# Attention value products with two heads in one strip of 32 rows, and two transposes per block in place of four

## Chip, cores and metric

The kernel runs on one core of a Trainium2 chip. The metric is device time in microseconds (us) of one execution. Engines: PE is TensorE (matmuls; PEld is its weight loads), DVE is VectorE, ACT is ScalarE, POOL is GpSimd, SP is SyncE, which issues most DMAs.

## The reference, cut to what matters

`x` has the shape 16 x 256 x 128 and is float32. Three layers follow one another: half a mixture-of-experts layer (8 experts, 2 per token), an attention layer, and the same half expert layer again.

```
x = x + 0.5 * ffn(layernorm(x))
x = x + attention(layernorm(x))
x = x + 0.5 * ffn(layernorm(x))

# attention: 16 heads of 8 values, chunks of 64 queries; each looks at its own chunk's keys and the chunk before
scores = einsum('bcqhd,bckhd->bchqk', qc, kc) * scale
attn   = softmax(where(valid, scores, -1e9))
out    = einsum('bchqk,bckhd->bcqhd', attn, vc) @ Wo.T + bo
```

## The kernel before, in words

The 4096 tokens are 32 tiles of 128 tokens (`T` = 32). Both expert layers (`ffn(0)`, `ffn(1)`) sort the tokens by expert through DRAM. Between them stands the attention, a software pipeline over the 32 tiles, here called blocks, with `T + TAIL` = 39 iterations of `attend(i)` on each engine. The order of work on each engine is written out by hand, and semaphores join the engines. Two blocks are one sequence (`TS` = 2): t even is its first block, t odd its second.

PE's iteration i (L785) goes, in this order:

1. `round_one(i)` (L637): scores of block i+1 for the strips 2 and 3 (L624) and transposed scores of block i-1 (L628). It waits for `m01_ready`, so that the maxima of the last scores are read out of PSUM, and for `p01_ready`.
2. `small_moves(i)` (L719): three 128x128 products or transposes (L724, L727, L730), one of which transposes `OS`, the finished heads' output of block i-3.
3. `values(i-2)` (L761): the value products of block i-2.
4. `round_two(i)` (L656, lines L628 and L634), `router_part(i)` (L740: in three of four iterations a piece of the second router, with the lines L518, L526 or L535; all of them write the same PSUM bank `M1`, after a wait for `pvs_ready`), and `round_three(i)` (L670, lines L634 and L624).
5. `stage(i)` (L698): values, queries and keys of a sequence to come (L705, L711 or L716, L717).
6. `to_tokens(i-2)` (L733): after a wait for `pvs_ready`, four 128x128 transposes (L737) from `PVS` into `M1`.

The value products: the probabilities `PT` lie with keys on the 128 partitions and queries along the free dimension, and the values `VM` are the stationary operand. In `VM` each head owns 32 columns: 8 values, a one (whose product is the sum of the probabilities), and 23 zeros. A product of a head therefore gives 32 rows of PSUM, of which 9 are used. `M1` is one PSUM bank of 512 columns. Head b*4+h writes the rows of strip h (32h to 32h+31) and the columns of b (128b to 128b+127), so that 16 heads fill the bank. An even block takes 16 matmuls of 128 columns (L780), an odd one 32 of 64 columns (L782); four consecutive ones go to the four strips.

ACT then copies `M1` (128x512) to `PVS` (L975), PE transposes its four squares back into `M1` (L737), and DVE's `divide` (L1280) takes the reciprocals of the 16 sums (L1285) and multiplies (L1286) into `OS`, which raises `os_ready`. `values` of the next block waits for `os_ready`.

DVE's iteration (L1289): `maxima(i, 0)` (L1278) after `round_three`, `divide(i-3)`, at some iterations the combination of the first expert layer's results (L1250) or parts of the router, `maxima(i+1, 2)` (L1278) after `round_one` of the next iteration, the rest of that work, and the residual addition (L1325). ACT's iteration (L959): the copy of the small moves (L964), at some iterations normalised rows (L942) or a copy of rows (L880), the copy to `PVS` (L975), the exponentials (L922) in two halves, and copies for `stage`.

Of the kernel before, what the change touches and what calls it, by code (L numbers as in the profile page):

```python
# [24 lines left out]
P = 128  # L25
# [4 lines left out]
H, DH, W = 16, 8, 64  # L30
C = L // W
TS = L // P
ROWS32 = 32
HG = P // ROWS32
HQ = H // HG
KINDS = 4
QRING = 6
KRING = 3
# [28 lines left out]
def need(eng, sem, value):  # L67

    if not (isinstance(value, int) and value <= 0):
        eng.wait_ge(sem, value)  # L70
# [31 lines left out]
def macaron(nc, x, wq, bq, wk, bk, wv, bv, wo, bo, rscale, rw, experts, pes, consts, picks, out):  # L102
# [8 lines left out]
    with ExitStack() as ctx:  # L111
        def sb(name, shape, dt=F32):
            return ctx.enter_context(nc.sbuf_tensor(name, shape, dt))

        def sem(name):
            return ctx.enter_context(nc.semaphore(name))
# [11 lines left out]
        o = 0  # L128
# [4 lines left out]
        IDN, BEFORE, ONES, HMASK, IOTA, REG0, KTH, SIOTA, TRI, SROW, TOKEN, FROW = parts  # L133
# [6 lines left out]

        VM = sb("VM", [P, KRING, 3, H * ROWS32])
        MB = [sb(f"MB{i}", [P, P]) for i in range(2)]
        PT = [sb(f"PT{i}", [P, HG, KINDS * P]) for i in range(2)]
        MOP = [sb(f"MOP{i}", [P, 3, P]) for i in range(2)]
        PVS, RD, OS = sb("PVS", [P, HG, P]), sb("RD", [P, H]), sb("OS", [P, H, DH])
        CW = sb("CW", [P, T, TOPK])
        NHALF, REPS, EULER = sb("NHALF", [P, T]), sb("REPS", [P, T]), sb("EULER", [P, T])
        FILL = sb("FILL", [P, FILLERS, D + 1])
# [44 lines left out]
        ABANK = [PS[:, i, :] for i in range(2)]  # L193
        BBANK = [PS[:, 2 + i, :] for i in range(HG)]
        M0, M1 = PS[:, 6, :], PS[:, 7, :]
        EARLY = PS[:, 4, :]

        ROUTER = [PS[:, 4, :], PS[:, 5, :], PS[:, 6, :]]
# [40 lines left out]
        p01_ready, p23_ready, pv_done, pvs_ready = sem("p01_ready"), sem("p23_ready"), sem("pv_done"), sem("pvs_ready")  # L239
        to_done, os_ready, res_done = sem("to_done"), sem("os_ready"), sem("res_done")  # L240
# [27 lines left out]
        def two_halves(bank, v):  # L268
            return bank[:, v * P:(v + 1) * P].rearrange("p (a q) -> p a q", q=W)

        def moved(i):


            return [n for n, t in enumerate((i, i - 3, i - 4)) if blk(t)]
# [92 lines left out]
        def _(pool):  # L367
# [6 lines left out]
            pool.wait_ge(vm_zeroed, 1)  # L374
            pool.memset(VM[:, :, :, :].rearrange("p s w (h c) -> p (s w h) c", c=ROWS32)[:, :, DH:DH + 1], 1.0)\
                .then_inc(vm_zeroed, 1)
# [134 lines left out]
        def _(pe):  # L511
# [29 lines left out]
            def ffn(ph):  # L541
# [50 lines left out]
                for s in range(WRITTEN[ph] * XRING):  # L592
# [3 lines left out]
                    if ph == 0 and s in (10, 12, 14):  # L596
                        i = s // 2 - 9
                        stage_bank_free(i)
                        stage(i, EARLY)
                with pe.Fori(WRITTEN[ph], n // XRING - 1) as i:  # L600
# [6 lines left out]
            def strip(a):  # L607
                return slice(a * ROWS32, (a + 1) * ROWS32)

# [5 lines left out]
            def own_twice(t, a):  # L615
                return K[strip(a), t // TS % KRING, 0:W].unsqueeze(1).broadcast_to([ROWS32, 2, W])

# [68 lines left out]
            def stage_bank_free(i):  # L686


                s, odd = i // TS + 1, i % TS
                if odd:  # L690
                    if seq(s + 1):
                        pe.wait_ge(xat_ready, s + 2)
                    elif seq(s):
                        pe.wait_ge(v_ready, s + 1)
                elif seq(s):
                    pe.wait_ge(k_ready, s + 1)

            def stage(i, bank=M0):  # L698


                s, odd = (i + 1) // TS + 1, (i + 1) % TS
                if odd:
                    if seq(s):
                        for a in range(TS):
                            ins = pe.matmul(bank[:, a * P:(a + 1) * P], XAT[:, a * P:(a + 1) * P], WV[:, :],  # L705
                                            start=True, stop=True)
                    if seq(s + 1):
                        if (s + 1) * TS % TG == 0:
                            pe.wait_ge(xa_ready, (s + 1) * TS // TG + 1)
                        for a in range(TS):  # L710
                            ins = pe.transpose(bank[:, L + a * P:L + (a + 1) * P], XA[:, (s + 1) * TS % TG + a, :], IDN)  # L711
                    if seq(s) or seq(s + 1):
                        ins.then_inc(vx_done, 1)
                elif seq(s):
                    pe.wait_ge(xat_ready, s + 1)
                    pe.matmul(bank[:, 0:L], WQ[:, :], XAT[:, :], start=True, stop=True)  # L716
                    pe.matmul(bank[:, L:2 * L], WK[:, :], XAT[:, :], start=True, stop=True).then_inc(qk_done, 1)  # L717
# [15 lines left out]
            def to_tokens(t):  # L733

                pe.wait_ge(pvs_ready, t + 1)
                for b in range(HG):
                    ins = pe.transpose(M1[:, b * P:(b + 1) * P], PVS[:, b, :], IDN)  # L737
                ins.then_inc(to_done, 1)

            def router_part(i):  # L740
# [20 lines left out]
            def values(t):  # L761


                s, a = t // TS, t % TS
                pe.wait_ge(p23_ready, t + 1)
                if a == 0:
                    pe.wait_ge(v_ready, s + 1)
                else:
                    pe.wait_ge(vm_ready[s % KRING], 16 * 2 * (s // KRING + 1))
                need(pe, os_ready, t)  # L770
                for b in range(HG):
                    p = PT[t % 2][:, b, :].rearrange("p (r h q) -> p r h q", r=2, q=W)
                    out = two_halves(M1, b)
                    for r in (None,) if a == 0 else (0, 1):
                        w = 0 if a == 0 else 2 if r == 0 else 1
                        for h in range(HQ):
                            o = (b * HQ + h) * ROWS32
                            v = VM[:, s % KRING, w, o:o + ROWS32]
                            if r is None:
                                ins = pe.matmul(out[strip(h), :, :], v, p[:, :, h, :], start=True, stop=True)  # L780
                            else:
                                ins = pe.matmul(out[strip(h), r, :], v, p[:, r, h, :], start=True, stop=True)  # L782
                ins.then_inc(pv_done, 1)

            def attend(i):  # L785
# [86 lines left out]
        def _(act):  # L872
# [9 lines left out]
            def ffn(ph):  # L882
# [21 lines left out]
                for s in range(written):  # L904
# [3 lines left out]
                    if ph == 0 and s in (11, 13, 15):  # L908
                        stage((s - 1) // 2 - 9, EARLY)
                with act.Fori(written // RING, n // RING - 1) as i:  # L910
# [33 lines left out]
            def attention_rows(g, half=None):  # L944

                act.wait_ge(lnshift_ready, g + 1)
                for a in range(TG) if half is None else range(half * TG // 2, (half + 1) * TG // 2):
                    ins = normalised(XA[:, a, :], g * TG + a, LN, a)
                if half != 0:
                    ins.then_inc(xa_ready, 1)  # L950
# [8 lines left out]
            def attend(i):  # L959
                if moved(i):  # L960
                    act.wait_ge(mt_done, i + 1)
                    need(act, res_done, i - 5)
                    parts = slice(moved(i)[0] * P, (moved(i)[-1] + 1) * P)
                    act.copy(MOP[i % 2][:, :, :].rearrange("p n q -> p (n q)")[:, parts], M0[:, parts]).then_inc(mt_ready, 1)  # L964
                if i == 0:
                    attention_rows(1)
                if (g := group(i, 5)) is not None:
                    attention_rows(g)
                if (g := group(i, -8)) is not None:
                    router_inputs(g)  # L970
                if (g := group(i, -9)) is not None:
                    second_rows(g)
                if blk(i - 2):
                    act.wait_ge(pv_done, i - 1)
                    act.copy(PVS[:, :, :].rearrange("p b q -> p (b q)"), M1).then_inc(pvs_ready, 1)  # L975
                if blk(i - 1):
                    act.wait_ge(r2_done, i)
                    probabilities(i - 1, 0).then_inc(p01_ready, 1)
                if (g := group(i, -8)) is not None:
                    router_rows(GROUPS + g, M1, XNT[:, :])  # L980
                if blk(i - 1):
                    act.wait_ge(r3_done, i + 2)
                    probabilities(i - 1, 1).then_inc(p23_ready, 1)
                stage(i)
# [47 lines left out]
        def _(dve):  # L1032
# [247 lines left out]
            def divide(t):  # L1280


                dve.wait_ge(to_done, t + 1)
                o = M1.rearrange("p (h c) -> p h c", c=ROWS32)
                step(dve.reciprocal(RD[:, :], o[:, :, DH]))  # L1285
                dve.tensor_tensor(OS[:, :, :], o[:, :, 0:DH], RD[:, :].unsqueeze(2).broadcast_to([P, H, DH]),  # L1286
                                  ALU.mult).then_inc(os_ready, 1)
# [222 lines left out]
```

## Time and profile before

| what | us |
|---|---|
| median of 3 runs (lowest to highest) | 640.94 (639.59 to 642.64) |
| the profiled execution's own time | 640.15 |
| its span, first to last instruction | 638.1 |
| PE busy | 520.2 (82%) |
| PE weight loads busy | 457.1 (72%) |
| DVE busy | 416.4 (65%) |
| ACT busy | 277.3 (43%) |
| POOL busy | 363.3 (57%) |

By the trace the attention's value products run from 235.9 to 455.8 us. Before them lie the first router and expert layer, and behind them the second expert layer and the last combination. "Idle before" in a row is the time for which the engine did nothing ahead of the instruction, and the arrow names who ended it; "issue" means that the profile shows nobody. Rows of one engine can overlap, since matmuls are pipelined.

### The profile page before, as it was taken

Reading aid. Unit: us, or ns where it says so; the run is one execution under the profiler, and the core shown is the slowest. Engines: PE = TensorE matmul, PEld = TensorE weight load, DVE = VectorE, ACT = ScalarE, POOL = GpSimd, SP = SyncE. Lnnn points to the kernel's source line nnn. Section 1 sums busy time; section 2 is a strip of 40 time slices with the busy share of each in tenths; the row PEclk is TensorE's granted clock in tenths of the full one; section 3 lists DMA queues with packets and bytes.
Section 4 is the critical chain, followed back from the end, with each engine's and each line's share of the span. In section 5 each row is a group of like instructions: output and inputs, shape, how many; then the busy total and the mean of one; then the engine's idle time right before and its main releaser. Section 6 shows DMA issues by size and latency. Waiting matters only on the chain.

```text
span 638.1 us, 20679 instructions
## 1 busy us (share of the span) xinstructions
PE 520.2 (82%) x7242; PEld 457.1 (72%) x7243; DVE 416.4 (65%) x1431; ACT 277.3 (43%) x627; POOL 363.3 (57%) x425
## 2 busy tenths in 40 slices
PE   0899865999999599999999899999730999999920
PEld 0666635899999478888788778878520999999920
DVE  5776653666676857677688887656324566766747
ACT  0444112443443246666566657555420344434404
POOL 8777775775566431343657565561667556656630
PEclk9999896999999679999899999999855899999975
DMA  9611222222322312010212111120102222323259
GB/s 268 206 48 54 68 70 51 84 71 83 83 82 75 100 51 66 23 52 20 76 30 76 35 40 33 44 55 19 34 27 77 72 81 85 83 74 92 83 143 277
DMA packets 60136, 49.37 MB, mean 77 GB/s; under 512 B 8736, under 2 KB 53536, under 8 KB 59936
## 3 DMA queue, kind: packets, MB, share of 16 engines
q1 hardware_dynamic: 51872, 31.51, 18.6%
q0 software_dynamic: 8192, 16.86, 8.0%
q8 instruction: 50, 0.82, 0.5%
q14 instruction: 22, 0.18, 0.1%
HBM read 23.55 MB, written 20.59 MB: 69 GB/s over the span
## 4 chain that ended last, share of the span: by engine, by line
PE 57%; DVE 13%; POOL 10%; issue 8%; DMA 5%; ACT 3%; SPq 3%; DVEq 0%; POOLq 0%; ACTq 0%
PE PS L560 16%; PE PS L574 7%; PE PS L634 7%; POOL xs_rows L408 6%; PE PS L628 5%; DVE MB L1278 4%; DVE X L1250 4%; PE PS L526 3%; PE PS L549 3%; PE PS L782 2%; POOL ys_rows L423 2%; PE PS L818 2%; DMA XS<-xs_rows 2%; PE PS L624 2%; DMA ys_rows<-YO,XS 1%
## 5 line engine op out<-in xcount | busy, mean ns | idle before, releaser
L423 POOL DMA_INDIRECT ys_rows<-YO,XS x136 | 130.9, 963 | 89.5 <-issue 54.5
L560 PE MATMUL PS<-XST,WG 128*128 128x128 f32 x1088 | 151.3, 283 | 0.0
L408 POOL DMA_INDIRECT xs_rows<-XN,IDX x120 | 118.0, 984 | 36.2 <-issue 34.1
L560 PEld LDWEIGHTS PS<-XST,WG 128*128 128x128 f32 x1088 | 134.9, 195 | 3.9 <-issue 0.2
L1179 DVE TENSOR_TENSOR AV<-PS,GA 128x256 f32<-128x256 f32 x136 | 57.7, 424 | 85.5 <-PE PS L574 43.1
L1278 DVE TENSOR_REDUCE MB<-PS 128x8 f32<-128x1024 f32 x64 | 78.2, 1222 | 42.7 <-PE PS L624 42.4
L893 ACT ACTIVATE GA<-PS 128x256 f32<-128x256 f32 x136 | 52.1, 383 | 95.7 <-PE PS L560 95.5
L574 PE MATMUL PS<-EXP,AV 128*128 x544 | 83.2, 276 | 1.3 <-DVE AV L1179 1.2
L628 PE MATMUL PS<-QM,K 32*128 32x128 f32 x1024 | 76.8, 287 | 5.8 <-DVE MB L1278 4.2
L922 ACT ACTIVATE PT<-PS 128x1024 f32<-128x1024 f32 x64 | 64.4, 1022 | 31.0 <-PE PS L624 17.4
L634 PE MATMUL PS<-MOP,PICKS 32*128 32x128 f32 x1024 | 74.7, 287 | 0.9 <-issue 0.8
L628 PEld LDWEIGHTS PS<-QM,K 32*128 32x128 f32 x1024 | 64.7, 190 | 12.3 <-issue 12.3
L574 PEld LDWEIGHTS PS<-EXP,AV 128*128 128x128 f32 x544 | 71.7, 192 | 1.9 <-issue 1.9
L634 PEld LDWEIGHTS PS<-MOP,PICKS 32*128 32x128 f32 x1024 | 64.2, 192 | 7.6 <-issue 5.5
L1188 DVE COPY WG<-EXP 128x512 f32 x136 | 64.5, 475 | 4.6 <-issue 1.8
L888 ACT COPY XST<-PS 128x128 f32<-128x128 f32 x136 | 36.1, 266 | 66.6 <-PE PS L549 63.0
L549 PE MATMUL PS<-CN,XS 128*128 128x128 f32 x136 | 39.9, 293 | 29.6 <-DMA XS<-xs_rows 27.5
L624 PE MATMUL PS<-K,QM 32*128 32x128 f32 x768 | 60.2, 290 | 4.1 <-DVE MB L1278 4.1
L624 PEld LDWEIGHTS PS<-K,QM 32*128 32x128 f32 x768 | 51.4, 198 | 5.0 <-DVE MB L1278 4.4
L452 POOL TENSOR_TENSOR QM<-QS,CN 128x256 f32<-128x256 f32 x64 | 38.4, 630 | 22.1 <-ACT QS L937 21.9
L549 PEld LDWEIGHTS PS<-CN,XS 128*128 128x128 f32 x136 | 19.6, 144 | 34.0 <-issue 29.9
L381 POOL TENSOR_TENSOR rstd_rt<-vareps_rt,NHALF 128x4 f32<-128x4 f32 x8 | 8.3, 1035 | 60.3 <-DVE vareps_rt L1054 60.3
(172 smaller groups left out, 882.0 us busy)
## 6 DMA issues: line engine op xcount, KB each, us to landing
XS<-xs_rows SPq DMA_DIRECT2D x136, 64.5 KB, 1.8
VM<-VM SPq DMA_DIRECT2D x32, 128.0 KB, 2.4
XN<-ys_rows SPq DMA_DIRECT2D x16, 256.0 KB, 5.4
YG<-ys_rows SPq DMA_DIRECT2D x14, 256.0 KB, 2.8
EXP<-experts SPq DMA_DIRECT2D x1, 3072.0 KB, 11.2
ys_rows<-YO,XS POOLq DMA_INDIRECT x136, 2.2
X<-x SPq DMA_DIRECT2D x4, 512.0 KB, 6.3
xs_rows<-XN,IDX POOLq DMA_INDIRECT x120
```

What stands on the lines that cost most here:

```text
L408: pool.indirect_dma_start(xs, bass.IndirectOffsetOnAxis(ap=IDX[:, place, c, i:i + 1], axis=0), XN[:, c, place, i, :], None).then_inc(scatt ...
L423: pool.indirect_dma_start(ys, bass.IndirectOffsetOnAxis(ap=XS[:, r, D:D + 1].bitcast(U32), axis=0), YO[:, r, :], None).then_inc(ys_out[r], 16)
L549: pe.transpose(XTP[r % 2], XS[:, r, 0:D], IDN).then_inc(xt_done, 1)
L560: ins = pe.matmul(HPS[r % 2][:, c * P:(c + 1) * P], WG[r % 2][:, c * P:(c + 1) * P], XST[r % 2][:, :], start=True, stop=True)
L574: ins = pe.matmul(YPS[r % 2], AV[r % 2][:, c * P:(c + 1) * P], EXP[:, bass.ds(o + (GW + c * D), D)], start=(c == 0), stop=(c == 1))
L624: return pe.matmul(ABANK[a % 2][:, v * P:(v + 1) * P], queries(t, a, v), window(t, a, v), start=True, stop=True)
L628: return pe.matmul(BBANK[a][:, v * P:(v + 1) * P], window(t, a, v), queries(t, a, v), start=(v == 0), stop=False, skip_group_check=True)
L634: return pe.matmul(BBANK[a][:, v * P:(v + 1) * P], SEL[strip(a), pick, :], MOP[t % 2][strip(a), 0, :], start=False, stop=True, skip_group_ ...
L922: return act.activation(PT[t % 2][:, 2 * half:2 * half + 2, :], PS[:, 2 + 2 * half:4 + 2 * half, :], ACT.Exp)
L1179: dve.tensor_tensor(AV[r % 2][:, :], HPS[r % 2][:, HID:GW], GA[r % 2][:, :], ALU.mult)\
L1188: dve.tensor_copy(WG[r % 2][:, :], EXP[:, bass.ds(o, GW)]).then_inc(wg_ready, 1)
L1278: return dve.tensor_reduce(out, PS[:, 0:2, :].rearrange("p a (v k) -> p a v k", k=P), AX_X, ALU.max, negate=True)
```

## The change

It touches the value products, the copy of their result, the transposes back and the addresses that `divide` reads. Heads 8b+2h and 8b+2h+1 now share strip h in the columns of b, with b = 0, 1. The weights of the second head of such a pair start 16 columns earlier in `VM`: they take 16 zero columns of the head before, then its own 8 values, its one and 7 zeros, so that its result lies in rows 16 to 24 of the strip. The first head's product fills rows 0 to 8 (with zeros below), and the second is added to it in PSUM. Only the first matmul of each strip has `start` set. The products fill 256 columns of `M1` (`PAIRED`), and the two transposes write the other 256 (`TOKENS`).

```diff
+HALF = ROWS32 // 2
...
-        PVS, RD, OS = sb("PVS", [P, HG, P]), sb("RD", [P, H]), sb("OS", [P, H, DH])
+        PVS, RD, OS = sb("PVS", [P, 2, P]), sb("RD", [P, H]), sb("OS", [P, H, DH])
...
+        PAIRED, TOKENS = M1[:, 0:2 * P], M1[:, 2 * P:4 * P]
...
             def to_tokens(t):
 
                 pe.wait_ge(pvs_ready, t + 1)
-                for b in range(HG):
-                    ins = pe.transpose(M1[:, b * P:(b + 1) * P], PVS[:, b, :], IDN)
+                need(pe, os_ready, t)
+                for b in range(2):
+                    ins = pe.transpose(TOKENS[:, b * P:(b + 1) * P], PVS[:, b, :], IDN)
                 ins.then_inc(to_done, 1)
...
                 need(pe, os_ready, t)
-                for b in range(HG):
-                    p = PT[t % 2][:, b, :].rearrange("p (r h q) -> p r h q", r=2, q=W)
-                    out = two_halves(M1, b)
-                    for r in (None,) if a == 0 else (0, 1):
-                        w = 0 if a == 0 else 2 if r == 0 else 1
-                        for h in range(HQ):
-                            o = (b * HQ + h) * ROWS32
-                            v = VM[:, s % KRING, w, o:o + ROWS32]
-                            if r is None:
-                                ins = pe.matmul(out[strip(h), :, :], v, p[:, :, h, :], start=True, stop=True)
-                            else:
-                                ins = pe.matmul(out[strip(h), r, :], v, p[:, r, h, :], start=True, stop=True)
+                for b in range(2):
+                    for second in range(2):
+                        for r in (None,) if a == 0 else (0, 1):
+                            w = 0 if a == 0 else 2 if r == 0 else 1
+                            for h in range(HQ):
+                                x = b * 2 * HQ + 2 * h + second
+                                p = PT[t % 2][:, x // HQ, :].rearrange("p (r h q) -> p r h q", r=2, q=W)[:, :, x % HQ, :]
+                                out = two_halves(PAIRED, b)[strip(h)]
+                                if r is not None:
+                                    p, out = p[:, r, :], out[:, r, :]
+                                o = x * ROWS32 - second * HALF
+                                v = VM[:, s % KRING, w, o:o + ROWS32]
+                                ins = pe.matmul(out, v, p, start=(b == 0 and second == 0 and r != 1), stop=True,
+                                                skip_group_check=True)
                 ins.then_inc(pv_done, 1)
...
-                    act.copy(PVS[:, :, :].rearrange("p b q -> p (b q)"), M1).then_inc(pvs_ready, 1)
+                    act.copy(PVS[:, :, :].rearrange("p b q -> p (b q)"), PAIRED).then_inc(pvs_ready, 1)
...
-                o = M1.rearrange("p (h c) -> p h c", c=ROWS32)
+                o = TOKENS.rearrange("p (h c) -> p h c", c=HALF)
```

## Rows read from the trace of the kernel before

**Rows 1.** Attention: length; busy PE, PEld, DVE, ACT, POOL (count); granted clock, DMA share, GB/s.
```profile
234.00:448.00 214.00, 203.21 (x4766) 174.91 (x4767) 153.42 (x475) 132.32 (x236) 105.72 (x153) 0.99 0.16 43
```
**Rows 2.** Groups of instructions by line and shape: busy us, mean ns, idle before.
```profile
L1278 DVE TENSOR_REDUCE MB<-PS 128x8 f32<-128x1024 f32 x64 | 78.2, 1222 | 42.7 <-PE PS L624 42.4
L628 PE MATMUL PS<-QM,K 32*128 32x128 f32 x1024 | 76.8, 287 | 5.8 <-DVE MB L1278 4.2 <-issue 0.5
L634 PE MATMUL PS<-MOP,PICKS 32*128 32x128 f32 x1024 | 74.7, 287 | 0.9 <-issue 0.8
...
L737 PE MATMUL PS<-CN,PVS 128*128 128x128 f32 x128 | 19.9, 279 | 0.4 <-issue 0.4
L975 ACT COPY PVS<-PS 128x512 f32<-128x512 f32 x32 | 18.5, 577 | 8.0 <-PE PS L780 5.3 <-PE PS L782 2.5
...
L780 PE MATMUL PS<-PT,VM 128*32 128x128 f32 x512 | 17.3, 276 | 0.0
...
L933 ACT COPY XAT<-PS 128x256 f32<-128x256 f32 x16 | 6.3, 391 | 0.0
```
**Rows 3.** Timeline at the end of an odd iteration: start us, us, engine, line.
```profile
307.07 1.23 DVE L1278 TENSOR_REDUCE MB<-PS 128x8 f32<-128x1024 f32 x1
...
307.70 0.60 PE L737 MATMUL PS<-CN,PVS 128*128 128x128 f32 x4
...
308.41 0.22 PEld L628 LDWEIGHTS PS<-QM,K 32*128 32x128 f32 x2 [0.35 <-issue]
```
**Rows 4.** The same at the ends of the first and the last of twelve even iterations.
```profile
245.10 1.22 DVE L1278 TENSOR_REDUCE MB<-PS 128x8 f32<-128x1024 f32 x1 [2.19 <-PE PS L624]
...
246.44 0.21 PEld L628 LDWEIGHTS PS<-QM,K 32*128 32x128 f32 x2 [0.17 <-issue]
246.55 0.26 DVE L1285 RECIPROCAL RD<-PS 128x16 f32<-128x16 f32 x1 [0.23 <-PE PS L737]
...
419.49 1.22 DVE L1278 TENSOR_REDUCE MB<-PS 128x8 f32<-128x1024 f32 x1 [1.70 <-PE PS L624]
...
420.84 0.20 PEld L628 LDWEIGHTS PS<-QM,K 32*128 32x128 f32 x2 [0.17 <-issue]
```
**Rows 5.** Waits over the whole span: us in total, times, longest us.
```profile
PEld PS L518 <- ACT PVS L975: 4.5, 7, 0.7
```
**Rows 6.** Timeline where DVE's maxima start late.
```profile
252.20 1.23 DVE L1278 TENSOR_REDUCE MB<-PS 128x8 f32<-128x1024 f32 x1
...
253.54 0.22 PEld L628 LDWEIGHTS PS<-QM,K 32*128 32x128 f32 x2 [0.81 <-issue]
```
**Rows 7.** Timeline: PE's wait for the router's sums in an iteration with prefixes.
```profile
352.11 0.30 PEld L535 LDWEIGHTS PS<-IND,CN 128*128 128x128 f32 x2 [1.18 <-issue]
```
**Rows 8.** Timeline of the attention's last iterations.
```profile
441.89 1.16 PE L628 MATMUL PS<-QM,K 32*128 32x128 f32 x16
...
453.84 0.26 DVE L1285 RECIPROCAL RD<-PS 128x16 f32<-128x16 f32 x1 [3.40 <-PE PS L737]
...
456.80 0.97 PEld L526 LDWEIGHTS PS<-RWS,XNT 128*128 128x128 f32 x8 [0.89 <-ACT PVS L975]
...
458.26 1.09 PE L737 MATMUL PS<-CN,PVS 128*128 128x128 f32 x4 [0.40 <-issue]
```
**Rows 9.** Busy time by engine before and where the granted clock falls.
```profile
308.00:314.00 6.00, 5.09 (x140) 4.24 (x138) 4.23 (x17) 2.59 (x7) 2.71 (x5) 1.00 0.33 86
314.00:320.00 6.00, 6.00 (x80) 5.09 (x80) 2.52 (x12) 2.51 (x4) 3.97 (x5) 0.72 0.08 25
```
**Rows 10.** Timeline of the same stretch.
```profile
316.53 1.23 DVE L1278 TENSOR_REDUCE MB<-PS 128x8 f32<-128x1024 f32 x1 [1.66 <-PE PS L624]
...
318.19 0.60 PE L737 MATMUL PS<-CN,PVS 128*128 128x128 f32 x4
```
**Rows 11.** Timeline: the transposes around an iteration with router logits at full clock.
```profile
339.07 0.60 PE L737 MATMUL PS<-CN,PVS 128*128 128x128 f32 x4
...
346.70 0.60 PE L737 MATMUL PS<-CN,PVS 128*128 128x128 f32 x4
```

## The prediction
> **What bounds the kernel now.** I read the busy times by stretch first. In the attention's steady part PE is busy for 203.21 of 214 us [rows 1], so that at first sight every matmul taken off PE is time won. The groups by line give the prices [rows 2]. The timeline then has to say what PE waits for just behind the four transposes that the change halves, for only there can their going be seen.
>
> At the end of an iteration two things run side by side. `round_three` has ended; DVE reads the new scores for the maxima (1.22 us [rows 2]), while PE does `stage` and the four transposes. The next `round_one` overwrites those scores and waits for the maxima. In the odd iteration the maxima end at 307.07 + 1.23 = 308.30, the transposes end at 308.30 too, and the next load comes at 308.41 with 0.35 us of idle before it [rows 3]. In the even one the maxima end at 246.32 and the load comes at 246.44, 0.12 behind; in the last of the twelve that I read it is 420.71 and 420.84, 0.13 [rows 4]. In the twelve the distance is 0.11 to 0.15 us, and in the odd ones 0.11 or 0.12. So 0.11 us is what the release costs, and DVE's maxima set the start of `round_one` almost everywhere, by nearly the same time as the transposes. The transposes are covered by the maxima. PE is busy without being the bound at this spot.
>
> **The change part by part.**
>
> Value products: as many matmuls as before (16 or 32), of the same columns and strips, in sets of four strips. Taken at nothing added. No row shows a second head added onto a strip in this shape. The nearest is L634, which adds onto scores that L624 and L628 have written, at a mean of 287 ns against 287 for L628, which doesn't add onto an earlier product [rows 2]. Lower bound: nothing, as the columns streamed are the same; upper bound: see the third rival. I take the value of the nearest row.
>
> Two transposes fewer per block. Four take 0.60 us from start to end with the last one's 0.27 us included, so a transpose comes every 0.11 us; two are 0.22 us, over 32 blocks 7.0 us. What of it counts:
> - Odd iterations: nothing, since 0.35 us of idle stood there already [rows 3]. It becomes 0.57.
> - Twelve even iterations: only what the distance has over 0.11 us. The sum over the twelve is 0.2 us.
> - The iteration in which the clock was low: the maxima end at 317.76 and the transposes at 318.79 [rows 10], so the transposes do set it: 0.2 us.
> - The last iterations, where no scores are left and no maxima cover them: `round_one` at 441.89 stands right behind the transposes (0.22 us); DVE's reciprocal at 453.84 waits for them, and the small moves for it (0.22); those at 458.26 take 1.09 us, so two are 0.5 us [rows 8]. Together 0.95 us. The set at 446.7 in between I cost at nothing: a chain over DVE and POOL towards the next router is later there.
>
> `divide` starts earlier. In even iterations DVE waits 0.23 us for the transposes ahead of the reciprocal [rows 4]; with two gone this wait is nearly gone, and all that DVE has in that iteration moves up by 0.2 us. It counts where DVE is late: the maxima at 252.20 follow DVE's own work and not PE, and `round_one` waits 0.81 us for them [rows 6]: 0.2 us. PE's wait for the router's sums, 1.18 us at 352.11 [rows 7], stands twice with that length (0.4 us) and three times with about 0.2 us (0.1 us in all). Two more late maxima lie in iterations counted under the copy, and are not counted twice. In `divide` itself only the distance between elements changes, 16 for 32; taken at nothing, with 0.05 us a block as bound either way, which the cover of the maxima takes up in most iterations.
>
> The copy to `PVS` falls from 128x512 to 128x256. The 128x512 takes 577 ns and the nearest 128x256 copy from PSUM 391 [rows 2], so about 0.2 us each. In most blocks ACT waits after it for `round_two` anyway, and nothing is won. PE itself waits for the copy ahead of the router's transposes seven times, with 4.5 us of load idle [rows 5], and once ahead of the logits at 456.80 [rows 8]: 8 x 0.2 = 1.6 us. Each of those waits is longer than 0.2 us, so the gain is whole. Behind it comes `round_three` and then the maxima, so it is passed on.
>
> The added wait in `to_tokens` for `os_ready` costs nothing: `values` of the same block has already waited for that value on the same engine, so nothing queued behind it is held. No DMA, and nothing on SP's and POOL's queues, is added or moved. What is late next after each gain is again the maxima.
>
> Sum: 0.2 + 0.2 + 0.95 + 0.2 + 0.5 + 1.6 = 3.65, say 3.7 us. The profiled execution took 640.15 us, 0.79 less than the median, so 3.7 us less is 636.45 on its scale and 637.2 on the median's. About half a per cent (3.2 us, below 637.7) is also what a measurement of this kernel can tell from no change, so the forecast lies just beyond that line.
>
> At the boundary the row says that the load follows the maxima by 0.11 us in even and odd iterations alike [rows 3, 4]. The Trainium skill, TensorEngine Tiling (Array Packing), section Tiling Modes, says that changing the tiling mode drains TensorE, and `round_one` has another mode than the transposes. By that rule the even iterations' 0.17 us of idle would be the drain behind the last transpose; this trace can't tell the two apart there, and what it would give is the first rival.
>
> **The rivals.**
>
> First, the even iterations are held by PE's own queue behind the last transpose, and the release of the maxima can come sooner than 0.11 us. Then up to 0.2 us more is won in each of twelve: 637.2 - 2.4 = 634.8. For it: the even idle is 0.17 us each time [rows 4]. Against it: the wait for the maxima is in the program, and their end lies only 0.12 us ahead. Chance 0.05. The bound beyond it, all 7.0 us plus 0.5 and 1.6, would be 631.8; the idle of the odd iterations excludes it.
>
> Second, the clock. In one iteration the granted clock fell from its level of 2.4 GHz to the one of 1.2 GHz for a part: its mean is 0.72 from 314 to 320 us, after 6 us in which it was full and PE was busy for 5.09 [rows 9]. The price: from 307.70 to 318.19 is 10.49 us between transposes [rows 3, 10], against 7.63 us from 339.07 to 346.70 in the same kind of iteration [rows 11], so one such fall costs 2.86 us with the stall that came with it.  The change adds 0.2 us of idle to most iterations, and every phase shifts. One fall more gives 640.05, chance 0.14; one fewer gives 634.35, chance 0.12.
> The Trainium skill, TensorE: Matmul & The Clock Gate, section Why this matters for your kernels, says that idle gaps between bursts of matmuls bring the clock down. It speaks against this change as far as the added idle goes; how long the gaps may be the rows here don't tell.
>
> Third, slower. The second head's matmuls write the addresses that the first head's have just written. If each such set of four had to wait until the set before had landed, about 0.27 us (L780's 276 ns [rows 2]) would come twice in an even block, where the two sets follow each other directly, and about 0.1 us twice in an odd one, where another set lies between. That is 16 x 0.54 + 16 x 0.2 = 11.8 us, on the path since nothing covers the value products: 637.2 + 11.8 = 649.0. It decides the sign from 0.22 us per block. Against it stand L634's rows, which show no such wait. Chance 0.07.
>
> Fourth, the gains are not passed on: behind each shorter wait stands another, and the time stays at 640 to 641. For it: PE and DVE end within 0.1 us of each other at many places. Chance 0.10. That the copy costs by instruction and not by columns, so that it does not shrink, would leave 638.8; the 577 against 391 ns speak against it, chance 0.02.
>
> **How the numbers follow.** The forecast has 0.50. Its own range, from the terms' bounds (a third of the 1.6 and of the 0.95 missing, or a further slice of the even iterations won), is 636.2 to 638.4, and about 0.32 of it lies below 637.7. Faster by over 0.5%: 0.32 + 0.12 + 0.05 = 0.49. Within 0.5%: 0.18 + 0.14 + 0.10 + 0.02 = 0.44. Slower: 0.07. The range takes in both falls of the clock and the unchanged time: 633.9 to 640.9; the third rival and part of the fourth are left out.
>
> **What would show it.** L737 has 64 instructions instead of 128, and two take about 0.38 us. The copy to `PVS` takes 0.37 to 0.40 us. In odd iterations the idle before `round_one` grows to about 0.57 us, in even ones to 0.37 to 0.40 us, and the load still follows the maxima by 0.11 us. The idle ahead of the router's transposes falls from 0.64 us on average (4.5 over 7) to about 0.44 us. The reciprocal follows the maxima without a wait in even iterations. The value products still take 1.08 us. If they take 1.3 us or more, or if the load follows the maxima sooner than 0.1 us, I am wrong at that step; if the clock falls another number of times inside the attention, the total is off by 2.86 us for each.

## The result, and the profile after

Over ten runs each, the changed kernel takes 636.04 us in the median (633.03 to 639.52) and the kernel before 640.66 us. The ratio is 0.9922, 95% interval 0.9893 to 0.9952: 5.0 us faster, or 3.1 to 6.9. A second comparison (`again`, below) gives 0.995, 0.9927 to 0.9973, so 3.2 us. The prediction was 3.7 us. The profiled execution took 636.84 us, with a span of 634.8. On two chips used below some executions ran in a slower state, and all medians, ratios and intervals here leave those out.

The groups by line of the changed kernel, with the lines that stand in place of those in [rows 2] (all line numbers are now a few higher: the maxima are L1283, the transposes L740, the copy to `PVS` L980, `divide` L1290, the value products L786):

```profile
L1283 DVE TENSOR_REDUCE MB<-PS 128x8 f32<-128x1024 f32 x64 | 78.2, 1222 | 41.9 <-PE PS L626 41.7
...
L786 PE MATMUL PS<-PT,VM 128*32 128x64 f32 x1024 | 17.6, 221 | 0.0
L786 PE MATMUL PS<-PT,VM 128*32 128x128 f32 x512 | 17.3, 276 | 0.0
L740 PE MATMUL PS<-CN,PVS 128*128 128x128 f32 x64 | 12.5, 277 | 0.4 <-issue 0.4
...
L980 ACT COPY PVS<-PS 128x256 f32<-128x256 f32 x32 | 11.6, 364 | 8.2 <-PE PS L786 8.0
```

The value products of 128 columns are busy for 17.3 us as before, at 276 ns: adding the second head onto the strip costs nothing, and a block's products take 1.08 to 1.11 us from first start to last end. There are 64 transposes, not 128, and the copy takes 364 ns in place of 577. PE is relieved of 7.4 us (19.9 to 12.5). Only part of it can be found in the time.

Where the rest went, the same odd iteration as in [rows 3] shows, in the timeline (start us, us, engine, line, and in brackets the idle time before):

```profile
306.20 1.23 DVE L1283 TENSOR_REDUCE MB<-PS 128x8 f32<-128x1024 f32 x1 [0.73 <-PE PS L626]
...
306.83 0.38 PE L740 MATMUL PS<-CN,PVS 128*128 128x128 f32 x2
...
307.54 0.22 PEld L630 LDWEIGHTS PS<-QM,K 32*128 32x128 f32 x2 [0.57 <-issue]
```

The maxima end at 307.43 and the load comes 0.11 us behind them, as before. The transposes end 0.22 us sooner and the idle ahead of `round_one` has grown from 0.35 to 0.57 us. The even iteration after it looks the same with 0.37 us of idle:

```profile
313.63 1.22 DVE L1283 TENSOR_REDUCE MB<-PS 128x8 f32<-128x1024 f32 x1 [0.87 <-PE PS L626]
...
314.46 0.38 PE L740 MATMUL PS<-CN,PVS 128*128 128x128 f32 x2
314.88 0.26 DVE L1290 RECIPROCAL RD<-PS 128x16 f32<-128x16 f32 x1
314.97 0.18 PEld L630 LDWEIGHTS PS<-QM,K 32*128 32x128 f32 x1 [0.37 <-issue]
```

DVE's reciprocal no longer waits for the transposes: it stands right behind the maxima, where [rows 4] had 0.23 us of idle ahead of it. Over all iterations with maxima the load follows them by 0.10 to 0.13 us.

The wait list of the changed kernel (us in total, times, longest us) has the copy's part, to be held against [rows 5], and the idle that the transposes left:

```profile
PEld PS L630 <- issue: 18.7, 32, 1.5
...
PEld PS L520 <- ACT PVS L980: 3.3, 7, 0.6
```

And the first of these two in the kernel before:

```profile
PEld PS L628 <- issue: 12.3, 33, 1.3
```

The wait ahead of the router's transposes went from 4.5 to 3.3 us. The idle ahead of `round_one`, of which the profile names no owner, went from 12.3 to 18.7 us. These 6.4 us of idle stand against the 7.4 us of which PE was relieved.

### The profile page after: what moved, and what is told of

Its sections match the earlier page's. It is cut to its first block, busy times and chain, and to the rows that moved or that the text cites. A ratio compares the mean times of both kernels' runs of the same rounds, so it can differ in the third digit from the quotient of the medians.

```text
span 634.8 us, 20565 instructions
## 1 busy us (share of the span) xinstructions
PE 513.5 (81%) x7178; PEld 450.8 (71%) x7179; DVE 417.5 (66%) x1431; ACT 271.1 (43%) x627; POOL 364.1 (57%) x425
## 3 DMA queue, kind: packets, MB, share of 16 engines
q1 hardware_dynamic: 51872, 31.51, 18.7%
## 4 chain that ended last, share of the span: by engine, by line
PE 56%; DVE 14%; POOL 9%; issue 8%; DMA 6%; ACT 3%; SPq 3%; DVEq 0%; POOLq 0%; ACTq 0%
PE PS L562 17%; PE PS L576 8%; POOL xs_rows L410 7%; PE PS L636 6%; DVE MB L1283 6%; PE PS L630 5%; DVE X L1255 3%; PE PS L786 3%; PE PS L551 3%; PE PS L528 3%; DMA ys_rows<-YO,XS 2%; PE PS L823 2%; ACT XN L947 2%; PE PS L626 2%; DMA XS<-xs_rows 2%
## 5 line engine op out<-in xcount | busy, mean ns | idle before, releaser
L1283 DVE TENSOR_REDUCE MB<-PS 128x8 f32<-128x1024 f32 x64 | 78.2, 1222 | 41.9 <-PE PS L626 41.7
L630 PEld LDWEIGHTS PS<-QM,K 32*128 32x128 f32 x1024 | 64.8, 190 | 18.9 <-issue 18.7
L636 PE MATMUL PS<-MOP,PICKS 32*128 32x128 f32 x1024 | 73.0, 285 | 0.1
L454 POOL TENSOR_TENSOR QM<-QS,CN 128x256 f32<-128x256 f32 x64 | 38.4, 630 | 20.1 <-ACT QS L942 19.9
```

Source lines behind the costliest of these rows:

```text
L630: return pe.matmul(BBANK[a][:, v * P:(v + 1) * P], window(t, a, v), queries(t, a, v), start=(v == 0), stop=False, skip_group_check=True)
L636: return pe.matmul(BBANK[a][:, v * P:(v + 1) * P], SEL[strip(a), pick, :], MOP[t % 2][strip(a), 0, :], start=False, stop=True, skip_group_ ...
L1283: return dve.tensor_reduce(out, PS[:, 0:2, :].rearrange("p a (v k) -> p a v k", k=P), AX_X, ALU.max, negate=True)
```

## The experiments

The theory to test, called the cover theory below: DVE's maxima cover the transposes, so that most of the 7 us is idle, and the gain comes from the shorter copy, the last iterations and DVE's earlier start. Against it stand "PE is the bound", by which every transpose counts, and "the clock", by which only fewer falls of the granted clock were won. Four kernels ran on one chip, beside one set of runs of the kernel before (median 639.42 us).

**The changed kernel once more** (`again`), no edit.

> The changed kernel once more, as the mark for the runs beside it. Cover theory (the transposes are covered by DVE's maxima; the gain comes from the shorter copy ahead of the router's transposes, the last iterations and DVE's earlier divide): 3 to 5 us faster than before. Rival 'PE is the bound' (every transpose counts): 7 to 9 us faster. Rival 'clock' (the gain is only fewer falls of the granted clock): 0 to 3 us, and the same spacing of the transposes in every iteration but those with a fall.

Measured: ratio 0.995, 0.9927 to 0.9973, 3.2 us. That is the cover theory's size, and less than half of what PE as the bound would give. This number alone does not exclude the clock, but the record of the runs speaks against it: the mean granted clock over the twelve runs is 0.919, and 0.920 over the 35 runs of the kernel before beside them. The changed kernel was not given a higher clock, so fewer falls are not the gain.

**The copy alone** (`four`):

```diff
+                for b in range(2):
+                    pe.transpose(PAIRED[:, b * P:(b + 1) * P], PVS[:, b, :], IDN)
                 for b in range(2):
                     ins = pe.transpose(TOKENS[:, b * P:(b + 1) * P], PVS[:, b, :], IDN)
```

> The changed kernel with two more transposes of the same data into the unused half of the bank, so four again; the copy stays short. Cover theory: the copy's part is left, 1.6 us faster than before, so 2 us slower than the changed kernel; the idle ahead of round_one is 0.35 us in odd and 0.17 us in even iterations again. PE is the bound: 7 us slower than the changed kernel, the time of before or more.

Measured: 0.9982, 0.995 to 1.0013, so 1.2 us faster than before, between 3.2 faster and 0.8 slower. That is 2.0 us slower than `again` by the two middle values, as forecast, and not 7: those would have put it 3.8 us above the kernel before, outside the interval. Set directly against `again`, by the means of the runs, it is 2.6 us slower, with an uncertainty of about 1.9 us either way. In its profile the idle ahead of `round_one` is 0.35 or 0.36 us in most odd iterations and 0.17 in the even ones, as forecast.

**The transposes alone** (`wide`):

```diff
-        PVS, RD, OS = sb("PVS", [P, 2, P]), sb("RD", [P, H]), sb("OS", [P, H, DH])
+        PVS, RD, OS = sb("PVS", [P, HG, P]), sb("RD", [P, H]), sb("OS", [P, H, DH])
...
-                    act.copy(PVS[:, :, :].rearrange("p b q -> p (b q)"), PAIRED).then_inc(pvs_ready, 1)
+                    act.copy(PVS[:, :, :].rearrange("p b q -> p (b q)"), M1).then_inc(pvs_ready, 1)
```

> The changed kernel with the copy to PVS of all 512 columns again, two transposes. Cover theory: PE waits 0.64 us per router transposes again, seven times, and the gain is what the transposes alone give, some 2 us faster than before. PE is the bound: 7 us faster than before.

Measured: 1.0009, 0.9985 to 1.0032: 0.6 us slower, between 1.0 faster and 2.0 slower. The 7 us are excluded; the 2 us forecast lie outside too, though not by much. The gain of the two parts alone, 1.2 and -0.6 us, adds up to 0.6 us and not to the 3.2 of both. A part of this may be the clock: the mean granted clock is 0.917 over the runs of `wide` and 0.918 over those of `four`, and among the runs of one kernel 0.001 more of it goes with some 0.5 us less. Taken at the clock of the kernel before, by this estimate, `wide` would be 1.1 us, `four` 1.4 and `again` 3.4 us faster than it. That is a correlation, and the rest of the gap stays open. Its waits have the copy's part back:

```profile
PEld PS L520 <- ACT PVS L980: 4.8, 7, 0.8
```

The lengths of single iterations, from one set of transposes to the next, separate the two parts better than the totals. In an iteration with the router's transposes it is 7.35 us in the kernel before (272.04 to 279.39) and 7.35 in `wide` (272.24 to 279.59), but 7.15 in `four` (272.92 to 280.07) and 7.14 in the changed kernel (271.70 to 278.84). The length follows the copy and not the number of transposes.

**Two transposes more than before** (`six`):

```diff
-                for b in range(HG):
+                for b in (0, 1) + tuple(range(HG)):
                     ins = pe.transpose(M1[:, b * P:(b + 1) * P], PVS[:, b, :], IDN)
```

> The kernel before with two transposes more, six per block. Cover theory, worked out from the distances at the ends of the iterations: even iterations have no room left, 13 x 0.22 us; odd ones have 0.18 us, 15 x 0.04; the last iterations and DVE's later divide 1.2 us: 4 to 5 us slower than before. So two transposes more cost more than two fewer give (2 us). PE is the bound: 7 to 8 us slower. If transposes don't matter: no change.

Measured: 1.0055, 1.0028 to 1.0083, 3.5 us slower (1.8 to 5.3); by the two medians it is 2.3 us. The middle value lies a little below the 4 to 5 us forecast. Two more cost time where two fewer (`wide`) gave none that could be measured. The timeline of an odd iteration, and of the even one behind it, says why:

```profile
263.47 1.22 DVE L1278 TENSOR_REDUCE MB<-PS 128x8 f32<-128x1024 f32 x1 [1.96 <-PE PS L624]
...
264.09 0.82 PE L737 MATMUL PS<-CN,PVS 128*128 128x128 f32 x6
264.84 0.19 PEld L628 LDWEIGHTS PS<-QM,K 32*128 32x128 f32 x2 [0.17 <-issue]
...
269.72 1.23 DVE L1278 TENSOR_REDUCE MB<-PS 128x8 f32<-128x1024 f32 x1 [0.80 <-PE PS L624]
...
270.53 0.82 PE L737 MATMUL PS<-CN,PVS 128*128 128x128 f32 x6
271.28 0.19 PEld L628 LDWEIGHTS PS<-QM,K 32*128 32x128 f32 x2 [0.17 <-issue]
```

At 270.95 the maxima are read and PE still has its transposes to do until 271.35: the load comes 0.33 us behind the maxima. In the odd iteration it comes 0.15 us behind them (264.69 to 264.84), where the 0.18 us of room have been used up. The start of `round_one` has moved back by about 0.2 us in even iterations and by 0.04 in odd ones. Room was there in one direction only.

**Shorter cover** (`before_half`, `after_half`): in both kernels the maxima are taken over every second key, so that DVE reads 512 elements a row and not 1024. The maxima of the other keys are left out.

```diff
-                return dve.tensor_reduce(out, PS[:, 0:2, :].rearrange("p a (v k) -> p a v k", k=P), AX_X, ALU.max, negate=True)
+                return dve.tensor_reduce(out, PS[:, 0:2, :].rearrange("p a (v k) -> p a v k", k=P)[:, :, :, 0:P:2], AX_X, ALU.max, negate=True)
```

> The kernel before with DVE's maxima over every second key only (512 elements a row instead of 1024), so that the cover is some 0.6 us shorter; the maxima over the other keys are left out. Cover theory: in odd iterations PE waits 0.18 us less, in even ones next to nothing, where DVE is late up to 0.6 us: 3 to 5 us faster than before. If maxima are the whole bound: 0.6 us in each of 32 iterations, 19 us faster.

> The changed kernel with the same shorter maxima. Cover theory: nothing covers the transposes now, so they count nearly in full: 7 to 9 us faster than the kernel before with the same shorter maxima (against some 4 to 5 us for the pair with whole maxima), and round_one starts 0.17 us behind the transposes' loads in odd iterations too. Rival 'PE is the bound': the same difference as the pair with whole maxima. Rival 'clock': the same.

**The router's transposes later** (`later`), a version that uses the idle which the change left:

```diff
-                if any(group(i, -lag) is not None for lag in (8, 9, 10)):
+                if any(group(i, -lag) is not None for lag in (9, 10)):
...
-                if (g := group(i, -8)) is not None:
-                    pe.wait_ge(px_used, len(SENT) + g)
-                    transposes_of_router(GROUPS + g, g, M1)
...
+            def router_part_late(i):
+                if (g := group(i, -8)) is not None:
+                    pe.wait_ge(*((pvs_ready, i - 1) if blk(i - 2) else (os_ready, T)))
+                    pe.wait_ge(px_used, len(SENT) + g)
+                    transposes_of_router(GROUPS + g, g, M1)
...
                 round_three(i)
+                router_part_late(i)
```

> The changed kernel with the router's four transposes of every fourth iteration behind round_three instead of ahead of it, so that the wait for the copy to PVS and the transposes themselves lie beside the maxima, where PE idles. Cover theory: 0.5 to 0.6 us less in each of seven iterations, 4 us faster than the changed kernel, 8 to 9 us faster than before. Rival: the copy of the transposed rows now delays the second half of the exponentials and holds up the transposes of to_tokens, and nothing is won, 0 to 2 us slower than the changed kernel.

These three ran on a chip on which every kernel is slower: the kernel before takes 722.63 us there. Measured: `before_half` 0.9871 (0.9788 to 0.9954), `after_half` 0.9758 (0.9668 to 0.9848), `later` 0.9813 (0.9749 to 0.9877), with medians of 712.92, 706.79 and 711.28 us. The changed kernel itself did not run beside them, so the same edits (`before_half2`, `after_half2` and `later2`) were measured once more with it (`again2`, no edit). Their chip is slow as well, with 708.23 us for the kernel before.

> The changed kernel as the mark for the three beside it: 0.3 to 0.8% faster than before.

> The kernel before with maxima over every second key, again, in case this chip is as quick as that of the first comparisons. Cover theory, from the periods of the regular iterations seen so far (6.22 instead of 6.45 us in odd, 6.00 instead of 6.22 in even ones): 4 to 6 us faster than before.

> The changed kernel with the same shorter maxima. Cover theory: the regular iterations are 0.22 us shorter than in before_half2, and the whole is 7 to 9 us faster than it. If the gain of the change is unconnected with the maxima: 3 to 5 us, as with whole maxima.

> The changed kernel with the router's transposes behind round_three. Cover theory: 0.5 us less in the iteration and 0.3 us in the next, seven times, 4 to 6 us faster than again2. Rival: nothing won, since the clock falls more often with the longer idle ahead of the scores or the second half of the exponentials comes late.

Measured: `again2` 0.9974 (0.9935 to 1.0013), `before_half2` 0.9879 (0.9837 to 0.9922), `after_half2` 0.984 (0.9786 to 0.9894), `later2` 0.9977 (0.9943 to 1.0011). The shorter maxima alone give 8.6 us (5.5 to 11.5) on the kernel before, and 9.3 (3.3 to 15.3) in the first comparison: more than the 4 to 6 and 3 to 5 forecast. By the medians the change is worth 4.0 us with shorter maxima (702.80 to 698.80; 2.8 by the ratios) against 1.4 with whole ones (708.23 to 706.88; 1.8 by the ratios); on the first of the two chips it was 6.1 us with shorter ones (8.2 by the ratios). The forecast was 7 to 9; the intervals are too wide to settle it from totals. The timelines settle what happens in the regular iterations. First `before_half`, the end of an even and of an odd iteration:

```profile
288.12 0.69 DVE L1278 TENSOR_REDUCE MB<-PS 128x8 f32<-128x512 f32 x1 [1.51 <-PE PS L624]
...
288.96 0.60 PE L737 MATMUL PS<-CN,PVS 128*128 128x128 f32 x4
289.49 0.19 PEld L628 LDWEIGHTS PS<-QM,K 32*128 32x128 f32 x2 [0.17 <-issue]
...
294.96 0.60 PE L737 MATMUL PS<-CN,PVS 128*128 128x128 f32 x4
295.49 0.19 PEld L628 LDWEIGHTS PS<-QM,K 32*128 32x128 f32 x2 [0.17 <-issue]
```

And the same of `after_half`:

```profile
288.14 0.69 DVE L1283 TENSOR_REDUCE MB<-PS 128x8 f32<-128x512 f32 x1 [1.01 <-PE PS L626]
...
288.95 0.38 PE L740 MATMUL PS<-CN,PVS 128*128 128x128 f32 x2
289.26 0.19 PEld L630 LDWEIGHTS PS<-QM,K 32*128 32x128 f32 x2 [0.17 <-issue]
...
294.74 0.38 PE L740 MATMUL PS<-CN,PVS 128*128 128x128 f32 x2
295.05 0.19 PEld L630 LDWEIGHTS PS<-QM,K 32*128 32x128 f32 x2 [0.17 <-issue]
```

The load now stands 0.17 us behind the last load of the transposes in all four, and 0.68 and 0.43 us behind the maxima at 288.81 and 288.83. From one iteration's transposes to the next it is 6.00 us with four of them (288.96 to 294.96) and 5.79 with two (288.95 to 294.74), and for the iteration behind it 6.22 and 6.00. So each is 0.21 to 0.22 us shorter, the whole price of two transposes. The pair `before_half2` and `after_half2` shows the same lengths: 6.00 and 6.22 against 5.78 and 6.01 us. With whole maxima the same two iterations take 6.00 and 6.45 us before and 5.98 and 6.45 after. It is the maxima that cover the transposes, and with half of them gone the transposes count.

`later` is 13.5 us (8.9 to 18.1) faster than the kernel before, more than the 8 to 9 forecast, but `later2` is no faster than `again2` (707.38 against 706.88 us), where 4 to 6 were forecast.

> The changed kernel with the router's transposes behind round_three, once more, for a chip on which the kernel before takes some 640 us. The traces on chips where it takes over 700 us show the iteration 0.55 us and the next 0.35 us shorter where DVE is in time, and nothing where DVE is late. Cover theory: seven times up to 0.9 us, 4 to 6 us on top of the change's own 3 to 5, so 1.2 to 1.6% faster than before. Rival (as on those chips): DVE's combination of the expert results is late in most of these iterations, and nothing is added to the change's 0.5 to 0.8%.

Measured: 0.9931, 0.9889 to 0.9973, on the chip of `later` once more, with 720.04 us for the kernel before; 1.2 to 1.6% had been forecast and 0.7% came. The ratios of the edit, 0.9813, 0.9977 and 0.9931, don't agree, the first and the last not even on one chip, and none was taken beside the changed kernel on a quick chip. Whether it beats the change stays open. In one pair of iterations of `later2` it does as forecast (6.58 and 7.27 us against 7.15 and 7.63 in `again2`); in others there DVE is late and the gain is lost.

## Why the prediction was right, point by point

**The forecast** was 3.7 us, the measurement 5.0 us (3.1 to 6.9) and 3.2 us (1.7 to 4.7) in two comparisons. The time lies in the range, on the side that was named, and the mechanism was the one described. How near the number came is partly luck: both intervals are about as wide as the forecast itself is large, and single terms missed by up to 0.2 us in both directions, as the points below show.

**Value products at nothing added.** Right: 17.3 us for those of 128 columns in both kernels. The third rival, slower by waits between the heads of a pair, is excluded: it wanted 0.54 us in an even block, and a block takes the same 1.08 us as before. One figure of that rival was wrong: a gain of 3.7 us over 32 blocks is used up at 0.12 us per block, not at 0.22.

**Transposes under the maxima.** Right, and shown from three sides: the idle grew by 0.22 us at unchanged distance from the maxima, two more transposes cost 3.5 us, and with shorter maxima each regular iteration is 0.21 to 0.22 us shorter. The first rival (the release could come sooner than 0.11 us) fell: in the changed kernel the distance is 0.10 to 0.13 us throughout, in even iterations too. (One odd iteration of the kernel before, at 280.11, stands at 0.13 us as well, where the prediction read 0.11 or 0.12 in all.) Behind the transposes PEld is idle for 0.17 us each time in `six` and in the pair with shorter maxima, and there this idle sets the start of `round_one`; where the maxima end later, they set it. By the rule of the Trainium skill, TensorEngine Tiling (Array Packing), section Tiling Modes, that changing the tiling mode drains TensorE, this idle would be the drain. The rows agree with that, but they don't show that the drain is its cause.

**The copy.** The duration was taken at 391 ns and is 364. PE's wait ahead of the router's transposes fell from 0.66 to 0.44 or 0.45 us six times, and not at all the seventh (0.59 and 0.60): 1.2 us in all (4.5 to 3.3). At 452.49 the wait ahead of the logits is 0.65 us against 0.89. The iteration of the seventh is 0.21 us shorter all the same (6.43 to 6.22), and so it is in `four` (6.23), but not in `wide` (6.43). The copy alone measured 1.2 us (3.2 faster to 0.8 slower) against the 1.6 forecast.

**The last iterations.** One of the term's three parts was wrong. The distance between the last two sets of transposes fell from 5.11 to 4.65 us, of which 0.24 is the wait for the copy ahead of the logits, so that the forecast 0.22 is left. The last transposes take 0.41 us and not 1.09, more than the 0.5 forecast; the pair at 459.05 in `wide` takes 0.59, so a part of this is the clock, which falls there in both kernels. The part behind 441.89 did not come. In the changed kernel:

```profile
437.67 0.44 PE L740 MATMUL PS<-CN,PVS 128*128 128x128 f32 x2
437.81 1.23 DVE L1283 TENSOR_REDUCE MB<-PS 128x8 f32<-128x1024 f32 x1 [0.45 <-PE PS L626]
...
438.95 0.25 DVE L1290 RECIPROCAL RD<-PS 128x16 f32<-128x16 f32 x1
439.57 0.14 PEld L729 LDWEIGHTS PS<-CN,OS 128*128 128x128 f32 x1 [0.31 <-DVE OS L1291]
```

`round_one` starts 0.22 us sooner here, but the small moves behind it wait for `divide`, and `divide` comes behind the last maxima on DVE. The prediction said that no maxima cover the transposes there. They do, by way of `divide`: the next set of transposes comes 5.41 us later in both kernels.

**DVE's earlier start.** The wait ahead of the late maxima near 252 was won (7.22 to 6.97 us for that iteration). The wait for the router's sums was counted as 0.5 us won over five iterations. Four of them are 0.36 us shorter together (6.87 to 6.78, 7.85 to 7.84, 7.85 to 7.69 and 6.89 to 6.79). In the fifth the wait grew. In the changed kernel:

```profile
316.55 2.32 POOL L454 TENSOR_TENSOR QM<-QS,CN 128x256 f32<-128x256 f32 x4
317.46 1.47 DVE L1095 TENSOR_TENSOR OH<-CN,TIX 128x32 f32<-128x32 f32 x2
...
319.88 0.30 PEld L537 LDWEIGHTS PS<-IND,CN 128*128 128x128 f32 x2 [1.19 <-issue]
```

And the same work in the kernel before, where POOL had finished by then:

```profile
320.08 1.18 POOL L452 TENSOR_TENSOR QM<-QS,CN 128x256 f32<-128x256 f32 x2
...
321.40 0.28 DVE L1090 TENSOR_TENSOR OH<-CN,TIX 128x32 f32<-128x32 f32 x2
...
322.63 0.30 PEld L535 LDWEIGHTS PS<-IND,CN 128*128 128x128 f32 x2 [0.23 <-issue]
```

The iteration takes 7.85 us in the changed kernel and 6.87 before. This is not the change's doing. In the kernel before, this is the iteration right behind the fall of the clock [rows 9], which had held PE back by 2.86 us, so that POOL was through with its multiplications when DVE came to the comparisons. `six`, whose transposes come later than before but whose clock did not fall there, shows the slow case:

```profile
317.38 2.32 POOL L452 TENSOR_TENSOR QM<-QS,CN 128x256 f32<-128x256 f32 x4
318.73 1.03 DVE L1090 TENSOR_TENSOR OH<-CN,TIX 128x32 f32<-128x32 f32 x2
```

Its iteration takes 7.84 us, as in `again` (7.86) and `wide` (7.84), which had no fall there either. `four`, which had one, takes 6.87. So such a fall gives 0.98 us back in the iteration behind it. Besides, some iterations moved by up to 0.9 us either way (7.99 to 8.73 and 7.36 to 6.43 in the changed kernel, and the same in `again`), for which no cause was shown.

**The clock.** The second rival put 2.86 us on each fall of the granted clock inside the attention. With the 0.98 us given back behind it, the fall in the kernel before cost 1.9 us. The one in `again`, in another iteration (8.36 us in place of 6.98), cost 1.4. The stretch from the first to the last transposes, in the busy times by stretch (length, then PE, PEld, DVE, ACT, POOL, granted clock), one row for each of the two kernels, the changed one second:

```profile
239.70:458.30 218.60, 205.99 (x4803) 176.88 (x4802) 153.45 (x482) 135.21 (x242) 110.91 (x157) 0.99 0.16 43
```

```profile
239.60:454.00 214.40, 197.16 (x4741) 168.38 (x4740) 154.86 (x482) 129.24 (x242) 110.68 (x157) 1.00 0.17 44
```

The stretch is 4.2 us shorter, at full clock. Of this 1.9 us are the fall, which the changed kernel's profiled execution happens not to have, and 2.3 are left. The profiles of the others have one fall (`again`, `four`), two (`wide`) and none (`six`). With each fall taken out at the length which the same iterations have elsewhere, the distance from the first to the last transposes is 216.7 us before, 214.3 in the changed kernel, 213.4 in `again`, 214.3 in `four`, 215.8 in `wide` and 220.6 in `six`. This is an estimate from one execution each, and the changed kernel and `again`, which are one program, differ by 0.9 us. The order is roughly that of the cover theory. Behind the attention the pair of profiles is a poor witness: from the start of the last transposes to the end it takes 179.8 us before and 180.9 after, where nothing was changed. Whether the added idle makes falls more frequent these few samples don't tell. The totals over many runs carry the verdict.

## What to carry to other kernels

Before counting what a removed instruction is worth, look at what its engine waits for next, and measure from the end of the covering work to the start of what follows: where this distance is the same in iterations with and without idle, the cover decides, not the engine. Two engines that end together are a bound in one direction only: less work on one gives nothing, and more work on it costs all that goes beyond the other's end. The shorter PSUM copy was won whole, 0.2 us, in most of the iterations in which PE waited for it. And when two profiles are compared, look for a stall in one of them first: it shifts the engines against each other, and the iteration behind it changes too.

## What was not expected of the hardware

Two comparisons on DVE with two operands in SBUF take 0.28 us together where POOL's multiplications are over and 1.47 us where POOL multiplies tensors at the same time, as the rows on the router's sums show (1.03 us in `six`, and 1.25 us at 349.92 in the kernel before, again beside POOL's multiplications); DVE's weighted sums, which have two operands in SBUF as well, vary alike (four take 1.13 us from 358.71, beside a POOL instruction of 4 columns, and 3.67 us from 360.89 in the changed kernel, where POOL's multiplications from 362.09 on fall among them). The Trainium skill, SBUF — State Buffer, section Who interferes with whom, says that a DVE instruction with two SBUF inputs contends with a GpSimd instruction that reads SBUF; these rows agree. Whether the two meet moves this iteration by 1 us.

The chips differ by more than any kernel here: the kernel before takes 639.42 us on one, 708.23 us on a second, and 722.63 and 720.04 us in two comparisons on a third. The cause was not looked for further.
